# Relative-position attention: one ring of transposes, minima instead of negated maxima, and band tiles moved in two narrower halves

## What is computed

```python
rel_k = pek[idx]                     # idx = clip(k - q, -128, 128) + 128
scores = einsum('bhqd,bhkd->bhqk', Q, K) / SCALE
scores = scores + einsum('bhqd,qkd->bhqk', Q, rel_k) / SCALE
scores = where(causal, scores, -inf)
attn = softmax(scores, axis=-1)
out = einsum('bhqk,bhkd->bhqd', attn, V)
out = out + einsum('bhqk,qkd->bhqd', attn, pev[idx])
```

## Time and profile before

| | us |
|---|---|
| median of 3 runs | 4722.8 (4718.19 to 4722.94) |
| the profiled execution | 4726.07 |
| its span, first to last instruction | 4724.3 |
| the stage `a2_soft` in it | 2545.6 to 3590.0 |

### The profile page before, as it was taken

One profiled execution on the slowest core, in us unless ns is written; L12 is line 12 of the kernel. 1 busy time (PEld: TensorE's weight loads), 2 busy tenths in 40 slices (PEclk: granted clock), 3 DMA queues, 4 the chain that ended last, 5 costly groups with the idle time before them and its releaser, 6 DMA issues. The chain is left out here.

```text
span 4724.3 us, 71233 instructions
## 1 busy us (share of the span) xinstructions
PE 3273.6 (69%) x22819; PEld 1813.4 (38%) x22883; DVE 2508.9 (53%) x5524; ACT 1860.5 (39%) x4386; POOL 682.5 (14%) x963
## 2 busy tenths in 40 slices
PE   5688554473526777777757777777774188859998
PEld 2344233352323444444434333333332022226776
DVE  4565466455645666666624555555555388821111
ACT  2355322220113555555533444444441177733332
POOL 2100000120003444444412000000000310000000
PEclk9798766686668999999976666766665599969999
DMA  4333000000001000000006777777673422220000
GB/s 128 54 53 56 20 0 0 8 1 5 0 28 27 17 17 17 17 17 17 17 22 190 216 215 211 214 208 213 206 216 91 128 46 49 45 68 1 0 0 18
DMA packets 419435, 337.10 MB, mean 71 GB/s; under 512 B 56079, under 2 KB 392138, under 8 KB 419154
## 3 DMA queue, kind: packets, MB, share of 16 engines
q1 hardware_dynamic: 409938, 312.39, 24.7%
q0 software_dynamic: 6912, 18.88, 1.3%
q10 hardware_dynamic: 2304, 2.36, 0.2%
HBM read 166.02 MB, written 150.22 MB: 67 GB/s over the span
## 5 line engine op out<-in xcount | busy, mean ns | idle before, releaser
L1214 DVE TENSOR_REDUCE a_soft_NM<-a_soft_s_ps 128x2 f32<-128x1024 f32 (+3 forms) x512 | 513.8, 1020 | 207.8 <-PE a_soft_s_ps L1149 138.2
L1248 ACT ACTIVATE a_soft_PTS<-a_soft_st_ps 128x512 f32<-128x512 f32 (+3 forms) x1024 | 458.5, 522 | 149.9 <-PE a_soft_st_ps L1125 104.6
L684 ACT ACTIVATE a_soft_PR<-a_soft_s_ps,a_soft_nmax 128x128 f32<-128x128 f32 (+3 forms) x512 | 269.9, 527 | 399.9 <-DVE a_soft_nmax L628 342.7
L485 PE MATMUL a_soft_pt_ps<-net_ident,a_soft_PR 128*128 128x128 f32 x1280 | 343.6, 383 | 9.7 <-ACT a_soft_PR L684 6.2
L1120 PE MATMUL a_soft_st_ps<-a_soft_QS,a_soft_KS 50*128 50x512 bf16 (+4 forms) x1024 | 257.9, 359 | 61.6 <-ACT a_soft_PTS L1248 33.2
L2043 DVE SCALAR_TENSOR_TENSOR net_X<-f_run_y_ps,f_COEF,net_X 128x128 f32 x256 | 72.1, 344 | 381.0 <-PE f_run_y_ps L2005 381.0
L2029 ACT ACTIVATE f_run_HT<-f_run_h_ps 128x512 f32<-128x512 f32 x256 | 153.0, 598 | 290.2 <-PE f_run_h_ps L1996 290.2
L2005 PEld LDWEIGHTS f_run_y_ps<-f_W,f_run_HT 128*128 128x128 f32 x2048 | 237.5, 192 | 26.8 <-issue 26.8
L1162 PE MATMUL a_soft_o_ps<-a_soft_PTS,a_soft_VR 128*32 128x512 f32 (+3 forms) x2048 | 242.6, 548 | 0.1
L2179 PE MATMUL f_run_ps<-f_run_WQKV,f_run_HT 128*128 128x512 f32 x384 | 226.9, 682 | 16.2 <-DVE f_run_RS L1477 8.3
L2005 PE MATMUL f_run_y_ps<-f_W,f_run_HT 128*128 128x128 f32 x2048 | 237.7, 275 | 0.0
(11 more groups left out here) (357 smaller groups left out, 6656.0 us busy)
## 6 DMA issues: line engine op xcount, KB each, us to landing
a_soft_BIAS<-skew_d SPq DMA_DIRECT2D x128, 512.0 KB, 4.7
band_d<-a_soft_PR SPq DMA_DIRECT2D x128, 512.0 KB, 3.6
skew_d<-a_soft_RS SPq DMA_DIRECT2D x128, 256.0 KB, 4.3
a_soft_PB<-band_d SPq DMA_DIRECT2D x128, 256.0 KB, 3.2
a_soft_QS<-query_rows_d SPq DMA_DIRECT2D x32, 384.0 KB, 9.5
query_rows_d<-a_proj_PARTS SPq DMA_DIRECT2D x72, 128.0 KB, 3.6
query_rows_d<-a_proj_PARTS POOLq DMA_DIRECT2D x72, 128.0 KB, 3.0
key_rows_d<-a_proj_PARTS SPq DMA_DIRECT2D x72, 128.0 KB, 3.9
```

The costliest lines, as they stand in the source:

```text
L485: last = pe.transpose(pt_ps[:, n % 2, kb * P:(kb + 1) * P], PR[:, n % NPR, OFF + kb * P:OFF + (kb + 1) * P], ident[:])
L684: act.activation(PR[:, n % NPR, OFF:OFF + w], s_ps[:, n % 4, 0:w], ACT.Exp, bias=nmax[:, n:n + 1]).then_inc(probs_ready, 1)
L1214: dve.tensor_reduce(NM[:, T % 2, j, p, :], s_ps[:, ring["s", a] % 2, :, 0:width(j)], AX.X, ALU.max, negate=True).then_inc(max_ready, 1)
L1248: act.activation(PTS[:, T % 2, 2 * p + par, kb, q0:S], st_ps[:, e % 3, q0:S], ACT.Exp, scale=scale).then_inc(probs_ready, 1)
```

## The change

`softmax_heads` becomes `relative_heads`, without the branches that this call did not take. In what runs, it does these things:

1. The turned band no longer goes to `r_ps` but to the two banks of `pt_ps`, in turn with the transposes of probabilities. A head has five groups in the order tile 2 of the head before, tile 3 of the head before, band of the head two before, tile 0, tile 1; the bank of group `pos` of head `h` is (5h + pos) % 2. Bank 0 is copied by VectorE, bank 1 by ScalarE, at fixed places behind the tile's reduction or exponential. `relative` waits only for ScalarE's copy of the relative scores before.
2. The queries are scaled by a negative factor, the mask's constant is positive, VectorE forms minima, and the exponential takes `scale=-1.0`. The negation (L628) and the drain ahead of it are gone.
3. The bias load and the band store move in two transfers each, rows 0 to 63 with columns 1 to 191 and rows 64 to 127 with columns 65 to 255, so rows of 764 B.
4. Before the stage's work GpSimd copies the mask `skew_base` into all of `BIAS` (128 partitions x 4096 f32), ahead of `init_done`; SP waits for `init_done` before the first bias load.

The core of the diff:

```diff
-    c["skew_base"] = np.where(kk <= q, 0.0, NEG).astype(np.float32)
+    c["skew_base"] = np.where(kk <= q, 0.0, -NEG).astype(np.float32)
+BIAS_WINDOWS = BAND_WINDOWS = [(0, P // 2, 1, 3 * P // 2 - 1), (P // 2, P // 2, P // 2 + 1, 3 * P // 2 - 1)]
...
-                sp.dma_start(BIAS[:, h, :, :], bass.AP(skew_d.tensor, h * TB * 2 * P * P, [[2 * P, P], [2 * P * P, TB], [1, 2 * P]])
-                             ).then_inc(bias_loaded[h], 16)
+                for r0, n, c0, m in BIAS_WINDOWS:
+                    sp.dma_start(BIAS[r0:r0 + n, h, :, c0:c0 + m], window(skew_d, h, r0, n, c0, m)).then_inc(bias_loaded[h], 16)
...
-                sp.dma_start(bass.AP(band_d.tensor, h * TB * 2 * P * P, [[2 * P, P], [2 * P * P, TB], [1, 2 * P]]),
-                               bass.AP(pr0.tensor, pr0.offset, [list(pr0.ap[0]), [OFF + S + P, TB], [1, 2 * P]])
-                               ).then_inc(band_stored[h], 16)
+                for r0, n, c0, m in BAND_WINDOWS:
+                    pr = PR[r0:r0 + n, 4 * (h % 2), c0:c0 + m]
+                    sp.dma_start(window(band_d, h, r0, n, c0, m),
+                                 bass.AP(pr.tensor, pr.offset, [list(pr.ap[0]), [OFF + S + P, TB], [1, m]])).then_inc(band_stored[h], 16)
...
+            pool.tensor_copy(BIAS[:].rearrange("p h j c -> p (h j) c"),
+                             bass.AP(skew_base[:].tensor, skew_base[:].offset, [list(skew_base[:].ap[0]), [0, 4 * TB], [1, 2 * P]]))
...
+            def turned_slot(qd, h, pos):
+                slot = (5 * h + pos) % 2
+                earlier = through(qd, h, pos)
+                if not (isinstance(earlier, int) and earlier <= 0):
+                    pe.wait_ge(pt_copied[slot], earlier)
+                return slot
...
+            def turn_band(visit, hb, h, now, pos=2):
+                pe.wait_ge(band_loaded[hb % 2], 16 * (2 * visit + hb // 2 + 1))
+                slot = turned_slot(now, h, pos)
+                for j in range(TB):
+                    last = pe.transpose(pt_ps[:, slot, j * P:(j + 1) * P], PB[:, hb % 2, j, :], ident[:])
+                last.then_inc(pt_ready, 1)
...
-                if not (isinstance(hd, int) and hd < 6):
-                    pe.wait_ge(band_copied, hd - 5)
...
+        def copies(eng, slot, qd, sl, n, prev):
+            h, j = n // 4, n % 4
+            items = {0: (0,), 1: (1,), 2: (2, 3), 3: (4,)}[j]
+            for pos in items:
+                if (5 * h + pos) % 2 != slot:
+                    continue
+                if pos == 2:
+                    if h >= 2 or prev:
+                        copy_out(eng, slot, qd, h, pos, sl if h >= 2 else 1 - sl, (h + 2) % 4, None)
+                elif n >= 2:
+                    copy_out(eng, slot, qd, h, pos, sl, (n - 2) // 4, n - 2)
+                elif prev:
+                    copy_out(eng, slot, qd, h, pos, 1 - sl, 3, n + 14)
...
-                        dve.tensor_tensor_reduce(win, win, BIAS[:, h, j, 2 * P - ww:2 * P], 1.0,
-                                                 far_max[:, n:n + 1] if w > ww else -3.0e38, ALU.add, ALU.max, nmax[:, n:n + 1])
-                        dve.drain()
-                        dve.tensor_scalar(nmax[:, n:n + 1], nmax[:, n:n + 1], -1.0, None, ALU.mult).then_inc(max_ready, 1)
+                    dve.tensor_tensor_reduce(win, win, BIAS[:, h, j, 2 * P - ww:2 * P], 1.0, far_least[:, n:n + 1] if w > ww else 3.0e38,
+                                             ALU.add, ALU.min, least[:, n:n + 1]).then_inc(least_ready, 1)
+                    copies(dve, 0, qd, sl, n, prev)
...
-                    act.activation(PR[:, n % NPR, OFF:OFF + w], s_ps[:, n % 4, 0:w], ACT.Exp,
-                                   bias=nmax[:, n:n + 1]).then_inc(probs_ready, 1)
+                    act.activation(PR[:, n % NPR, OFF:OFF + width(j)], s_ps[:, n % 4, 0:width(j)], ACT.Exp,
+                                   bias=least[:, n:n + 1], scale=-1.0).then_inc(probs_ready, 1)
+                    copies(act, 1, qd, sl, n, prev)
```

More of the change, by code:

```diff
@@ L309, in softmax_heads @@
-        pv_done, o_copied = s.sem("pv_done"), s.sem("o_copied")
+        scores_ready, least_ready, probs_ready = s.sem("scores_ready"), s.sem("least_ready"), s.sem("probs_ready")
+        pt_ready = s.sem("pt_ready")
+        pt_copied = [s.sem("pt_by_dve"), s.sem("pt_by_act")]
+        vr_ready, pv_done, o_copied = s.sem("vr_ready"), s.sem("pv_done"), s.sem("o_copied")
         o_stored = [s.sem("o_stored0"), s.sem("o_stored1")]
[L311 to L325, removed]
@@ L333, in batches, with loads_of @@
             for u in range(4):
                 quad(0, u, u > 0)
-            with eng.Fori(1, B - 1 if skew is not None else B) as b:
+            with eng.Fori(1, B - 1) as b:
                 for u in range(4):
                     quad(b, u, True)
-            if skew is not None:
-                for u in range(4):
-                    quad(B - 1, u, True)
+            for u in range(4):
+                quad(B - 1, u, True)
             last()
+        def loads_of(b, u):
+            return 16 * NDMA * (2 * b + u // 2 + 1)
@@ L510, in relative @@
                     pe.wait_ge(rel_copied, hd)
[L511 to L512 removed]
                 for j in range(TB):
[L514 removed]
+                    last = pe.matmul(r_ps[:, j * P:(j + 1) * P], q_blk(u % 2, h, j), rel_k[:], start=True, stop=True)
                 last.then_inc(rel_ready, 1)
[L517 to L524 removed]
             def quad(b, u, prev):
@@ L530, in quad @@
                 pe.wait_ge(opnd_loaded[sl], loads_of(b, u))
-                if full:
-                    if prev:
-                        pe.wait_ge(v_read, qd)
-                    for h in range(4):
-                        for j in range(4):
-                            c = (4 * h + j) * HD
-                            last = pe.matmul(v_ps[:, c:c + HD], q_blk(sl, h, j)[0:SPLITS * HD], masks["part_sum"][:],
-                                             start=True, stop=True)
-                    last.then_inc(v_ready, 1)
@@ L574, in quad @@
+                    if prev and n in (9, 10, 11, 12, 13):
                         pv(qd - 1, 1 - sl, n - 9)
             def last():
-                turn(4 * B - 1, 14)
-                turn(4 * B - 1, 15)
-                if skew is not None:
-                    turn_band(16 * B - 2, 2, 4 * B - 1, 16 * B)
-                    turn_band(16 * B - 1, 3, 4 * B - 1, 16 * B)
-                for kb in range(NPT):
-                    pv(4 * B - 1, 1, kb)
-            if skew is not None:
-                for hd in range(3):
-                    relative(0, 0, hd, hd)
@@ new lines, in last @@
+                turn(4 * B - 1, 15, 0, 1, 4 * B)
+                turn_band(4 * B - 1, 2, 0, 4 * B)
+                turn_band(4 * B - 1, 3, 0, 4 * B, 3)
+                for kb in range(NPT):
+                    pv(4 * B - 1, 1, kb, 0)
+            for hd in range(3):
+                relative(0, 0, hd, hd)
+            batches(quad, last, pe)
+        def copies(eng, slot, qd, sl, n, prev):
+            h, j = n // 4, n % 4
+            items = {0: (0,), 1: (1,), 2: (2, 3), 3: (4,)}[j]
[9 more added lines that the diff above has]
+                    copy_out(eng, slot, qd, h, pos, 1 - sl, 3, n + 14)
@@ new lines, in copy_out @@
+        def copy_out(eng, slot, now, h, pos, sl, head, n):
+            eng.wait_ge(pt_ready, before(4 * now + h, pos + 1))
+            if n in (0, 1) and not (isinstance(now, int) and now < 2):
+                eng.wait_ge(pv_done, now - 1)
+            if n is None:
+                dst, src = PTS[:, sl, head, 4, :], pt_ps[:, slot, :]
+            else:
+                j = n % 4
+                dst = PTS[:, sl, head, 0:j + 1, j * P:(j + 1) * P]
+                src = pt_ps[:, slot, 0:width(j)].rearrange("p (k q) -> p k q", q=P)
+            if slot:
+                eng.activation(dst, src, ACT.Copy).then_inc(pt_copied[1], 1)
+            else:
+                eng.tensor_copy(dst, src).then_inc(pt_copied[0], 1)
@@ L719, in last @@
                     act.wait_ge(o, 64 * 2 * B)
-            if skew is not None:
-                for hd in range(3):
-                    copy_rel(hd, hd, 0)
-            batches(act, quad, last)
+            for hd in range(3):
+                copy_rel(hd, hd, 0)
+            batches(quad, last, act)
 def project_out(nc, stage, X, out_d, w, bias, ones_row, full):
```

304 lines of the change are left out of this document (107 added, 197 removed).

## The result

The changed kernel took 4649.8 us (median of 4, 4641.2 to 4653.9) against 4722.9 us for the kernel before on the same chip: ratio 0.9839, 95% interval 0.9824 to 0.9853. It is 73 us faster, where 128 were forecast. The time lies inside the forecast's range of 4515 to 4685, but outside the 4570 to 4632 that its main account gave itself, and nearer to rival 2's 4669. The profiled execution took 4653.9 us, its span is 4652.1.

The account below looks back on a forecast made before the run. The prediction took a ring of waits through the one bank r_ps, 7.96 us a head, to bound the kernel. 131.4 us off and 3.6 on, 127.8 net, took 4722.8 to 4595 us, range 4515 to 4685.

Parts of the forecast that it names:

- main account: Compute rings through the two transpose banks set 6.9 us a head after the change: 4595 us, 4570 to 4632, chance 0.48.
- rival 2: Half transfers bind: runs of 58.6 ns or exposed issues, DMA ring 7.2 us, with jitter 7.5: 4669 us, chance 0.22.
- one ring, through the bank: Before the change, both hand-overs of bank r_ps lie in a ring of waits setting 7.96 us a head.
- the DMA ring: SP's queue, band store landing before the next round: 6.5 us a head before, some 6.5 after, under the compute ring.
- The new compute ring, 6.9 us: Two transpose banks: even heads 6.15 us, odd 6.8, mean 6.5, plus 0.4 for output products, output copy and issues.
- The wait at tile 1's transposes for ScalarE's copy: In odd heads TensorE would wait there for ScalarE's band copy, showing the 6.8 us ring.
- Two more issues, "nothing": SP's two extra transfers a head, 0.36 us each, charged nothing; 0.7 us if nothing were in flight.
- Start: GpSimd's mask copy ahead of init_done, charged 3.6 us, all on the path; 4.9 us as the other end.
- The sum: Over the stage, (7.96 - 6.9) x 124 = 131.4 us off, 3.6 us on, 127.8 us net.
- Rival 3: TensorE's granted clock rises from 0.66, rings come to 5.9 to 6.3 us: 4521 us, chance 0.15.
- Rival 4: 764 B runs at odd starts are split or done twice, DMA ring 9.5 us: 4920 us, chance 0.08.
- Rival 5: Freeing the bank finds an equal ring in ScalarE's order, 7.9 us: 4719 us, chance 0.07.

Follow-up runs that it names:

- experiment 4: The kernel before with only the narrow half transfers and GpSimd's mask copy added, old banks and negations kept: 4724.7 us, ratio 1.0008.
- experiment 9: The kernel before with only SP's order changed, the band's load moved behind relative store and bias load: 4708.3 us, ratio 0.9962.
- experiment 1: The changed kernel with bias load and band store each as one whole transfer of 128 rows by 256 columns: 4728.8 us, ratio 1.0013.
- experiment 5: The kernel before with only queries negated and minima formed, the negation and its drain removed: 4722.6 us, ratio 0.9990.
- experiment 8: The changed kernel with whole transfers and SP's order store relative, load biases, load band, store band: 4596.2 us, ratio 0.9721.
- experiment 10: Experiment 8 without GpSimd's copy of the mask into the bias tiles: 4595.5 us, ratio 0.9726.
- experiment 11: Experiment 10 with the output transfers issued by GpSimd in place of ScalarE: 4603.3 us, ratio 0.9751.
- experiment 12: The changed kernel with whole transfers and SP's order load biases, load band, store relative, store band: 4603.7 us, ratio 0.9739.
- experiment 2: The changed kernel with one narrow transfer, 128 rows by 191 columns, for the two halves; outer columns left out: 4655.7 us, ratio 0.9853.
- experiment 7: The changed kernel, halves kept, with SP's order load biases, load band, store relative scores, store band: 4634.1 us, ratio 0.9803.
- experiment 3: The changed kernel with two halves of rows, but all 256 columns in each: 4757.4 us, ratio 1.0076.

## Why the prediction was right, and where it was not

The direction and the range came true; the account behind 4595 us did not. The prediction had one ring, through the bank, set the period, with the DMAs hidden under it before and after. The runs show two rings of nearly equal length before, so that both had to be shortened, and after the change the DMA ring still sets the pace. That the change shortened both made the sign right. That the time lies inside the range is owed to rival 2, which had a DMA ring of about the right length and a chance of 0.22, and is luck for the main sum.

| SP's order | banks and transfers | us | period |
|---|---|---|---|
| old | old banks, whole | 4722.9 | 7.96 |
| old | old banks, narrow halves | 4724.7 | 7.94 |
| old | new banks, whole | 4728.8 | 7.97 |
| old | new banks, narrow halves: the change | 4649.8 | 7.42 |
| band last | old banks, whole | 4708.3 | 7.85 |
| band last | new banks, whole | 4596.2 | 6.98 |

**What bounds the kernel before: half right.** The ring through the one bank is real (experiments 4 and 9 stop at it), but it was not alone: the DMA ring was as long (experiments 1 and 5 stop at that one). The prediction took SP's wait for the band as hidden, since SP also waited for the exponentials. A queue that shows both waits, the second in 47 of 100 heads at that line, fits two rings of about 7.9 us.

**The new compute ring, 6.9 us: the number came true, its parts did not.** In the changed kernel it is covered. Where the DMA ring is out of the way, the period is 6.98, 7.03, 6.94 and 7.02 (experiments 8, 10, 11 and 12). In experiment 8 ScalarE's copies of the relative scores are, from the first head of a quad to the second and so on, 5.97, 6.45, 7.49 and 8.16 us apart (means of 27 quads). The first two have no output products; 6.5 was forecast for their mean, and it is 6.2. The last two hold the output products, the output's copy and its issues; these cost 1.6 us in each, 0.8 a head, where 0.4 was charged. That the two errors cancel is luck. The wait at tile 1's transposes for ScalarE's copy was named beforehand: it is 47.1 us of the 86.2 at this line. The other 38.9 stand at tile 0's, which the prediction didn't name.

**The DMA ring, 6.5 us, "under the compute ring": this step failed.** It is 7.4 us. For the kernel before the sum of run times gave 5.1 us of work and 1.4 empty. Its own rows held a better figure, not used: a DMA share of 0.71 of a period of 7.96 is 5.65 us of work, so 2.3 empty. For the changed kernel 0.74 x 7.42 is 5.5 us of work, 1.9 empty. Of the 0.9 us that the forecast lacked, 0.5 is empty time, taken from one gap, and 0.4 is work, since runs of 512 and 1024 B were priced in single windows of 4 us. The run of 764 B was not the fault: by the records of the single packets of 2700 to 3400 it took 45.9 ns on the mean, where 47 was put in and 58.6 was rival 2's. A run of 512 B took some 32 ns in place of 26.0, and one of 1024 B 51 to 52 in place of 47.2 (the kernel before and experiment 1). SP's rounds, from one load of the band to the next, show the ring: 7.3 to 7.8 us on the mean at each of the four places in a quad in the changed kernel, and 7.9 to 8.3 in experiment 1, but 5.9 to 7.9 in experiment 8, where compute leads.

**Two more issues, "nothing": wrong, in a small way here.** A pair of half transfers takes SP 1.25 to 1.27 us in the rows above, one whole transfer 0.36 to 0.42, so 0.8 to 0.9 us more at each step, 1.7 a head, and not 0.7. It lies under SP's wait for the landing: with one narrow transfer that wait grows from 2.76 to 4.1 us a head, and the period stays (experiment 2). Where the landing is hardly waited for any more, the halves cost 30 us (experiments 7 and 12); how much of that is issue time and how much slower runs, no experiment tells apart.

**Start: right.** The copy as the timeline of GpSimd has it in the changed kernel:

```profile
2550.39 3.60 POOL L425 COPY a_soft_BIAS<-a_skew_base 128x4096 f32<-128x4096 f32 x1
```

3.60 us to the digit. TensorE's first wait of the stage is 16.50 us in place of 12.92, and the fourth copy of relative scores starts 2.9 us later than before (2565.16 against 2562.23).

**The sum.** (7.96 - 7.42) x 124 = 67 us off in place of 131, some 3 on, 64 net; the spans differ by 72. The other 8 us lie behind the stage: from its last output copy to that of the fourth attention it takes 583.0 us in the changed kernel and 590.9 (4178.9 - 3588.0) before. In the other runs it is 582.2 to 583.9 with the new function (593.3 where GpSimd issues the outputs) and 589.4 to 591.5 with the old one. The place can be named. It is the statistics of the layer normalisation behind this attention, 32 instructions of VectorE on a line that no edit touches; first the kernel before, then the changed one:

```profile
3665.31 0.29 DVE L155 BATCH_NORM_STATS2 n_st<-net_X  x1 [0.42 <-issue]
```

```profile
3596.34 0.29 DVE L155 BATCH_NORM_STATS2 n_st<-net_X  x1 [0.18 <-issue]
```

VectorE stands 0.42 us ahead of each in place of 0.18, for nothing that the profile shows. Over all 128 of these instructions that idle time is 31.4 us in every profile with the old function and 23.7 in every one with the new. Why is open; no experiment aimed at it. These 8 us are also why experiment 1, whose stage is over 6 us longer, ends level.

**The rivals.** Rival 2, the halves bind, described what happened: SP's wait for the band stayed and its waits for the exponentials all but vanished; its ring of 7.2 us and jitter to 7.5 are near the 7.42, its 4669 us is 19 too slow, 8 of them the stage behind. Its sign in the runs, over 50 ns, did not come, and SP's wait did not grow; its cause was only half right: not the halves (experiment 2 has none), but any transfer set of this size in that order. The Trainium skill (DMA: Bandwidth & Descriptors, Rules for kernel authors) advises against two transfers to disjoint partition halves. At equal bytes the runs agree: 29 us lost (experiments 1 and 3), and 30 in the order of experiment 7 even with fewer bytes (7 and 12). As part of the change the halves still won, since they made the narrower rows possible while bytes bound. Rival 3 fell: the clock stayed at 0.67, and 0.68 even at a period of 6.98. Rival 4 fell: it needed 70 ns a run, and 45.9 were measured. Rival 5 fell for the changed kernel; an equal ring existed, but in the DMAs and not on ScalarE.

What is open: the changed kernel's narrow halves in the order of experiment 8, and a single narrow transfer in it, were not run.

## What to carry to other kernels

Before pricing a new ring, take the old one's work from busy share times period, and suspect every resource whose ring comes out near the period: freeing one of two equal rings gave nothing (experiments 1, 4, 5) or 0.4% (experiment 9), shortening both 1.6% (the change) to 2.8% (experiment 8). In a queue that issues transfers, don't put the wait for a store's landing directly behind the store; with two independent transfers between them the same bytes and engines ran some 133 us faster (experiments 1 and 8), more than the narrower transfers gained.

## What was not expected of the hardware

- Issue time did not follow the bytes: one half of 64 rows takes SP 0.61 us (median), with rows of 764 B and of 1024 B alike (the change and experiment 3), and one transfer of 128 rows 0.36 to 0.48 (medians, experiments 1, 2 and 8). A pair of halves is 1.25 us in the rows above.
- Two transfers by partitions slow a part of the runs: by the records of the single packets one of 1024 B took 61.6 ns on the mean in halves and 51.9 in one transfer (experiments 3 and 1), one of 764 B 45.9 and 42.7 (the change and experiment 2). The medians are the same, 46 and 36 ns; it is the slowest quarter that differs (69 ns and more against 46, at 1024 B).
- Runs of 764 B that begin 132 B into a row (experiment 2) cost next to nothing extra: a straight line between its own 512 B runs (31.4 ns) and the 1024 B runs of experiment 1 (51.9) gives 41.5 ns, an estimate, and they took 42.7.
- With the same whole transfers the DMA engines moved 210 GB/s in experiment 1 and 241 in experiment 8, which differ only in the order of SP's queue.
